# Two-layer recurrent and attention block: attention operands kept in DRAM as long rows per head, half-wide diagonal steps of two chunks joined, first transpose one step earlier

## The reference, cut to what matters

```python
# layer 1, B=4, S=2048, 16 heads, D_H=16, D_HR=8 (rotary), d_qk=24
Q = concat([Qc, rope(Qr)], -1)          # per head 16 + 8 rows
K = concat([Kc, rope(Kr)], -1)          # Kr is one set of 8 rows, the same for all heads
scores = clip(einsum('bhqd,bhkd->bhqk', Q, K), -80, 80)
scores = where(causal, scores, -inf)
weights = softmax(scores / sqrt(d_qk), axis=-1)
attn = einsum('bhqk,bhkd->bhqd', weights, V)
x = x + (attn @ W_O) * g                # g from the second gate
```

## Time and profile before

| | |
|---|---|
| median of three runs | 2309.38 us (2303.23 to 2310.4) |
| profiled execution, own time | 2303.42 us |
| its span | 2301.7 us |
| mean granted TensorE clock | 0.957 |
| busy, share of the span | PE 88%, DVE 76%, ACT 69%, PEld 39%, POOL 36% |
| DMA | 150477 packets, 165.72 MB, of which 127104 packets under 2 KB |

### The profile page before, as it was taken

How to read it: one execution, slowest core, us unless ns; L and a number is a source line. 1 busy time by engine, 2 the same in 40 slices (tenths; PEclk the granted TensorE clock), 3 DMA queues, 4 the chain that set the end, 5 groups by cost and what they waited for, 6 DMA issues and landing times. The chain is left out here.

```text
span 2301.7 us, 45469 instructions
## 1 busy us (share of the span) xinstructions
PE 2031.1 (88%) x18726; PEld 894.3 (39%) x18726; DVE 1740.6 (76%) x2557; ACT 1592.7 (69%) x1897; POOL 830.4 (36%) x653
## 2 busy tenths in 40 slices
PE   5999999999986887877988898999888999888987
PEld 2656556565653554554222222222222222222225
DVE  7776675766649999997778677888677887677777
ACT  5545464554535555555889898999888998888982
POOL 2635455354555666674111111111111111111108
PEclk9999999999997899898999999999999999999999
DMA  3001001010113434448343144442244432444228
GB/s 95 19 19 37 19 19 37 19 38 19 52 32 122 162 125 157 141 135 196 41 63 41 36 58 65 63 62 35 47 65 63 48 51 39 63 63 61 67 96 305
DMA packets 150477, 165.72 MB, mean 72 GB/s; under 512 B 12416, under 2 KB 127104, under 8 KB 150016
## 3 DMA queue, kind: packets, MB, share of 16 engines
q1 hardware_dynamic: 148240, 160.59, 32.6%
q10 hardware_dynamic: 2032, 2.24, 0.3%
HBM read 91.21 MB, written 71.57 MB: 71 GB/s over the span
## 5 line engine op out<-in xcount | busy, mean ns | idle before, releaser
L1635 DVE TENSOR_SCALAR c_probs<-c_probs 128x512 f32<-128x512 f32 (+3 forms) x1152 | 777.7, 709 | 268.0 <-ACT c_probs L1604 180.2
L1604 ACT ACTIVATE c_probs<-c_ps_b 128x1536 f32<-128x1536 f32 (+1 forms) x576 | 827.4, 1436 | 0.0
L1685 PE MATMUL c_ps_o<-c_probs,c_v 128*32 128x512 f32 (+3 forms) x5120 | 606.0, 551 | 69.3 <-issue 39.7
L1650 POOL TENSOR_SCALAR_AFFINE_SELECT c_probs<-c_probs 128x512 f32<-128x512 f32 x256 | 192.8, 764 | 952.1 <-DVE c_probs L1635 952.1
L1669 PE MATMUL c_ps_b<-c_qk 24*128 24x512 f16 (+3 forms) x5760 | 468.6, 353 | 23.6 <-issue 23.6
L1669 PE MATMUL c_ps_a<-c_qk 24*128 24x512 f16 (+3 forms) x1920 | 458.5, 350 | 33.8 <-ACT c_probs L1602 23.6
L1602 ACT ACTIVATE c_probs<-c_ps_a 128x512 f32<-128x512 f32 (+1 forms) x576 | 357.8, 621 | 127.1 <-PE c_ps_b L1669 127.0
L1669 PEld LDWEIGHTS c_ps_a<-c_qk 24*128 24x128 f16 x1920 | 140.0, 93 | 540.7 <-ACT c_probs L1604 346.4
L258 POOL TENSOR_TENSOR a_hidh<-a_hid,a_hidh 128x512 f16<-128x512 f32 x128 | 169.0, 1338 | 234.9 <-ACT a_hidh L356 231.0
L1685 PEld LDWEIGHTS c_ps_o<-c_probs,c_v 128*32 128x32 f32 x5120 | 109.5, 109 | 322.7 <-issue 142.3
L667 PE MATMUL a_ps<-a_xnh,a_w 128*128 128x512 f16 x768 | 172.0, 379 | 12.0 <-ACT a_hid L351 12.0
(11 more groups left out here) (242 smaller groups left out, 2884.8 us busy)
## 6 DMA issues: line engine op xcount, KB each, us to landing
v_d<-b_val SPq DMA_DIRECT2D x16, 1024.0 KB
c_v<-v_d SPq DMA_DIRECT2D x16, 1024.0 KB
rows<-in_x SPq DMA_DIRECT2D x16, 512.0 KB, 4.9
x_d<-rows_out SPq DMA_DIRECT2D x16, 512.0 KB, 3.2
rows<-x_d SPq DMA_DIRECT2D x16, 512.0 KB, 5.3
qc_d<-b_qc SPq DMA_DIRECT2D x32, 256.0 KB
kc_d<-b_kc SPq DMA_DIRECT2D x32, 256.0 KB
gate_d<-rows_out SPq DMA_DIRECT2D x16, 512.0 KB, 3.3
```

Of the source, the lines that this page charges most:

```text
L1604: nc.scalar.activation(probs[:, t % NPROB, PARTS[1], 0:width(t)], ps_b[:, t % 2, :, 0:width(t)], ACT.Exp, scale=unscale).then_inc(exp_b_do ...
L1635: nc.vector.tensor_scalar(tile, tile, P_MAX, P_MIN, ALU.min, ALU.max).then_inc(clip_done, 1)
L1650: pool.affine_select(out=tile, in_=tile, compare_op=ALU.is_ge, fill=0.0, base=0, pattern=[[0, GH], [1, P]], channel_multiplier=-1).then_in ...
L1685: mm = nc.tensor.matmul(ps_o[j * VW:(j + 1) * VW, first_query:first_query + w], v[:, kt, j * VW:(j + 1) * VW], probs[:, t % NPROB, j, at:a ...
```

## The change

1. **Layout in DRAM.** q and k go to one tensor `qk_d` [batch, head, 32 rows, q/k, half, 2048 tokens], so that a row of a head is 16 KB in one piece. Content rows are stored with four DMAs for q and four for k (by half and by block of 128 channels), the rotary rows of q with two, and those of k with two that write the same 8 rows for all 16 heads (a broadcast source). Values go to [batch, group, partition, key tile, 128], so that a partition's 8 KB of a group lie together. Stores per chunk: 13 in place of 7.
2. **Loads of a group.** Five DMAs in place of 17: one for each head (24 rows of 16 KB), one for the values (128 rows of 8 KB).
3. **Attention output.** `attn_d` becomes [head, 32 rows, tokens]. One DMA of 128 partitions stores a chunk (256 KB in place of 4 x 32 KB, rows without meaning included). The output stage loads each chunk with two DMAs, whose source is 8 heads x 16 rows and whose destination is 128 partitions.
4. **Steps.** The half-wide D2 steps of chunks 0 and 1 are joined to one step of full width, those of 2 and 3 likewise, so a group has 34 steps and there are 544. A joined step is the last of the even chunk. Its first half is multiplied by V in its own `values`; its second half belongs to the odd chunk and is multiplied in the `values` of the next step. The `probs` buffer of a joined step is therefore free one step later, and ACT waits for that (`consumed`).
5. **Order.** DVE takes the four tasks of a chunk one step earlier: ahead of the clips of e+2, e+3, e+4 and e+5. All steps have two clips of full width, as the full-width ones had before.

```diff
-        "qc": dram("qc_d", [BATCH, 2, DIM, SEQ], F16),
-        "qr": dram("qr_d", [BATCH, 2, HEADS * D_R, SEQ], F16),
-        "kc": dram("kc_d", [BATCH, 2, DIM, SEQ], F16),
-        "kr": dram("kr_d", [BATCH, 2, D_R, SEQ], F16),
-        "v": dram("v_d", [TOKENS, HEADS * VW]),
+        "qk": dram("qk_d", [BATCH, HEADS, VW, 2, 2, SEQ], F16),
+        "v": dram("v_d", [BATCH, GROUPS, P, KEYT, GH * VW]),
...
-        "attn": dram("attn_d", [DIM, TOKENS]),
+        "attn": dram("attn_d", [HEADS, VW, TOKENS]),
...
-                        sp.dma_start(d["qc"][b, h, :, t].rearrange("(m p) t -> p m t", p=P), qc[:, s, h]).then_inc(stored[s], 16)
+                        for m in range(KT):
+                            sp.dma_start(content[b, m, :, 0:D_H, 0, h, t], qc[:, s, h, m]).then_inc(stored[s], 16)
                     sp.wait_ge(kr_low, n + 1 + 1)
-                    sp.dma_start(d["kr"][b, :, :, t].rearrange("h p t -> p h t"), kr[:, s]).then_inc(stored[s], 16)
+                    for h in range(2):
+                        sp.dma_start(rotary[b, D_H:D_QK, :, 1, h, t],
+                                     kr[:, s, h:h + 1].to_broadcast([D_R, HEADS, CH])).then_inc(stored[s], 16)
...
+    for j in range(GH):
+        sp.dma_start(into.memory[VW * j:VW * j + D_QK], d["qk"][b, g * GH + j, 0:D_QK]).then_inc(into.loaded, 16)
+    sp.dma_start(into.v[:], d["v"][b, g]).then_inc(into.loaded, 16)
...
-    return t.rearrange("(k p) (n t) -> n p k t", p=P, t=CH)
+    return t.rearrange("(k e) r (n t) -> n k e r t", k=KT, t=CH)[:, :, :, 0:D_H]
...
+        at = len(fulls) // 2
+        return [(D0, TPC * c)] + fulls[:at] + [(D13, TPC * c)] + fulls[at:]
+
+    for g in range(BATCH * GROUPS):
+        for c in range(0, CPB, 2):
+            steps += [(g, c, kind, kt) for kind, kt in chunk_steps(c)]
+            steps += [(g, c, D2, TPC * c)]
+            steps += [(g, c + 1, kind, kt) for kind, kt in chunk_steps(c + 1)]
...
+            return [(c, kt + 2, 0, HALF, HALF), (c + 1, kt + TPC + 2, HALF, HALF, HALF)]
+        return [(c, kt, 0, CH, 0)]
+
+    def products(t):
+
+        now = pieces(t)[:1] if steps[t][2] == D2 else pieces(t)
+        if t and steps[t - 1][2] == D2:
+            return [(t,) + p for p in now] + [(t - 1,) + pieces(t - 1)[1]]
+        return [(t,) + p for p in now]
...
+    def consumed(t):
+
+        return t + 2 if steps[t][2] == D2 else t + 1
...
-                        act.wait_ge(pv_done, t - NPROB + 1)
+                        act.wait_ge(pv_done, consumed(t - NPROB))
...
-                for t in range(N + LAG + 4):
-                    for after, task in ((0, to_tokens), (1, reciprocal), (2, normalise), (3, to_channels)):
-                        if t - LAG - after in end_of:
-                            task(end_of[t - LAG - after])
+                for t in range(N + LAG + 3):
+                    for after, task in ((-1, to_tokens), (0, reciprocal), (1, normalise), (2, to_channels)):
+                        if t - LAG - after in end_at:
+                            task(end_at[t - LAG - after])
...
+                    for step, c, kt, at, w, first_query in products(t):
+                        e = g * CPB + c
+                        opens = len(opened) == e
+                        if opens:
+                            opened.append(t)
+                            if e:
+                                pe.wait_ge(tok_done, e)
```

More of the change, by code:

```diff
@@ L1492, in attention @@
     FULL, D0, D13, D2 = range(4)
[L1493 removed]
     def chunk_steps(c):
         fulls = [(FULL, kt) for kt in range(TPC * c)]
[L1498 to L1503 removed]
+        at = len(fulls) // 2
+        return [(D0, TPC * c)] + fulls[:at] + [(D13, TPC * c)] + fulls[at:]
+    steps = []
+    for g in range(BATCH * GROUPS):
[3 more added lines that the diff above has]
+            steps += [(g, c + 1, kind, kt) for kind, kt in chunk_steps(c + 1)]
     N = len(steps)
[L1505 to L1508 removed]
     LAG = 3
@@ L1514, in attention @@
     PARTS = (slice(0, 1), slice(1, GH))
+    HALF = CH // 2
     def pieces(t):
-        _, c, kind, kt = steps[t]
+        g, c, kind, kt = steps[t]
         if kind == D13:
-            return [(kt + 1, 0, CH - P, P), (kt + 3, CH - P, P, CH - P)]
+            return [(c, kt + 1, 0, CH - P, P), (c, kt + 3, CH - P, P, CH - P)]
         if kind == D2:
-            return [(kt + 2, 0, CH - 2 * P, 2 * P)]
-        return [(kt, 0, CH, 0)]
-    def width(t):
-        return CH - 2 * P if steps[t][2] == D2 else CH
-    diagonals = {FULL: (), D0: (0,), D13: (0, CH - P), D2: (0,)}
+            return [(c, kt + 2, 0, HALF, HALF), (c + 1, kt + TPC + 2, HALF, HALF, HALF)]
[5 more added lines that the diff above has]
+        return [(t,) + p for p in now]
+    ordered = [(steps[t][0], p[1], t) for t in range(N) for p in products(t)]
+    chunks = BATCH * GROUPS * CPB
+    end_of = {}
+    for g, c, t in ordered:
+        end_of[g * CPB + c] = t
+    ends = [end_of[e] for e in range(chunks)]
+    end_at = {t: e for e, t in end_of.items()}
+    assert len(end_at) == chunks
+    def consumed(t):
+        return t + 2 if steps[t][2] == D2 else t + 1
+    diagonals = {FULL: (), D0: (0,), D13: (0, CH - P), D2: (0, HALF)}
     masks = [0]
@@ L1663, in scores @@
                         pe.wait_ge(exp_a_done, t)
-                    for kt, at, w, first_query in pieces(t):
+                    for c, kt, at, w, first_query in pieces(t):
                         for i, (hk, hq) in enumerate(TERMS):
@@ L1753, in batch_stored @@
         def batch_stored(batches):
[L1755 removed]
+            return 16 * (batches * GROUPS * CPB // ahead.OUTS) + 16
         with nc.Block() as block:
@@ L1764, in _ @@
                 for s in range(ROWS, SLOTS):
-                    sp.dma_start(attn(s), attn_v[s]).then_inc(loaded[s], 16)
+                    for k in range(KT):
+                        sp.dma_start(attn(s)[:, k], attn_v[s, k]).then_inc(loaded[s], 16)
                 for s in range(ahead.OUTS):
```

89 lines of the change are left out of this document (36 added, 53 removed).

## The result

| | before | changed |
|---|---|---|
| median of the runs | 2309.89 us (2303.23 to 2312.94, 4 runs) | 2269.67 us (2265.95 to 2273.54, 4 runs) |
| ratio, 95% interval | | 0.983 [0.9803, 0.9857] |
| profiled execution, span | 2301.7 us | 2264.2 us |
| mean granted clock | 0.957 | 0.968 |
| DMA | 150477 packets, 165.72 MB | 118090 packets, 178.00 MB |

The account below looks back on a forecast made before the run. ACT, closely followed by PE, bounds the attention, with long idles when load bursts delay PE's instructions. Terms -70 - 2 + 11 + 3 = -58 us against 2303.4 gave 2245; half of a 6 us offset made it 2248, range 2200 to 2292.

Parts of the forecast that it names:

- What bounds the kernel: Attention: ACT leads PE by some 0.05 us a step; long idles, 89 us, come from PE's instruction fetch behind load bursts.
- Part 1: Group loads in attention: faster q/k and value transfers shorten the bursts, saving 70 us (0 to 89).
- the 20 us kept for the bursts that still hurt: Attention: of 89 us of long idles, 20 were assumed to remain, for the bursts latest to recover.
- Part 2: Attention steps: two fewer steps a group, offset by new waits at joined steps; -2 us in all (bounds -45 to +45).
- the first pair: First joined step of a group: DVE late with clips, masks and transpose, so ACT idles 2.3 us, against 1.27 in the second.
- the drift I had named: Attention: a drift of 0.01 to 0.02 us a step, given for most of the gap between computed and profiled stage time.
- my check of the stage: Attention: 16 groups of 64.9 us plus 89 us of idle give 1127, against 1149 us profiled.
- Part 3: Output stage: the attention load from 8 heads runs at half rate, 1.36 us more for each of 8 chunks, +11 us.
- Part 4: Stores of the projections: hidden until the last chunk, whose stores must land before the stage ends; +3 us (0 to 30).
- The sign that I had named for being wrong here: Projections: a stage longer than 386 us by more than 3 would show the forecast wrong.
- (a) to (d): Bursts stay as long, chance 0.12; values wait makes it slower, 0.08; everything hidden, 0.12; loads outlast the double buffer, 0.04.
- (a): Rival on the attention's group loads: bursts stay as long, only some 10 us of idle go, 2305 us; chance 0.12.

Follow-up runs that it names:

- e6: Kernel before, old layout, with a group's operand loads issued in four parts after successive chunks instead of all at once: 2218.73 us, ratio 0.9662.
- e8: Kernel before with q and k in 16 KB rows and the new attention output layout, values still in 512 B pieces: 2246.69 us, ratio 0.9781.
- f5: Changed kernel with the rotary rows of k stored once, so a head is loaded with three DMAs, not one: 2362.35 us, 1.0253 of the kernel before.
- e4: Changed kernel with DVE's transpose and the tasks behind it back at their old place, one step later: 2280.74 us, 0.9941 of the kernel before.
- e7: Kernel before with only the values in long rows of 8 KB: 2304.68 us, ratio 1.0028.
- e3: Changed kernel with five probability buffers in place of four and one x1 row fewer held ahead: 2234.66 us, 0.9701 of the kernel before.
- e5: Changed kernel with the attention's output in DRAM, its stores and its load as before: 2267.82 us, 0.9852 of the kernel before.
- f3: Kernel before's layout with joined steps, early transpose, five probability buffers and spread loads, first prefetched group included: 2188.39 us, ratio 0.9511.
- f4: Changed kernel with a group's loads spread over four chunks, the first prefetched group's too: 2249.28 us, 0.9781 of the kernel before.
- e1: Changed kernel's new DRAM layout with the 36 steps and task order of before: 2251.45 us, 0.9786 of the kernel before.

## Why the prediction was right or wrong

- **What bounds the kernel: right.** PE starves when a load burst stays slow for long. e6, e8 and f5 show it from three sides: cut short, shortened, and made long again. The reading behind it, instructions whose fetch stands behind the loads, was an inference; the q8 packets show it. The figure with it was wrong. I had counted 13 to 15 us from the burst's start; counted from the last q8 packet, PE mostly lasts 17 to 20 us. In e4 a burst began at 1581.8, 9.3 us after such a packet, and PE stopped already 8.8 us into it, for 3.7 us.
- **Part 1, -70 us: -69 measured** (excess 91.6 to 22.9), **partly by luck.** The rate, put at 150 GB/s, is 136 to 184. But the slow part, put at 10 to 12 us, took 15, and the whole burst 21 in place of some 15: in those 15 us some 2.4 MB moved, more than the 1.5 MB of q and k that I had priced. And the 20 us kept for the bursts that still hurt had no sum behind them; the same loads left 17.0 to 42.3 us in the other kernels. The reason given, more partitions in a DMA, stands beside the smaller number of DMAs (f5). The values' rows, which I had priced at a part of the gain, bring nothing (e7). The rule quoted from the Trainium skill, "SBUF — State Buffer", section "Door 1: The DMA port swizzle", agrees in direction with f5: 24 rows of a head at 136 to 184 GB/s, 16 and 8 rows at 82 to 135. It does not fix the size: the 117 GB/s of the old burst is above what it would give for four of 16 ports (an estimate of 109 GB/s by that page's 435), where I had taken the 85 alone as agreement.
- **Part 2, -2 us: +9 measured, and the step that failed is the conversion of idle into time.** The idles came out as worked: 1.26 + 1.20 in the first pair against 2.3, 1.19 in the second against 1.27, together 3.65 against 3.6. But three intervals of a group are longer by 1.51, 1.33 and 1.54 us, 4.4 in all, since a waiting exponential loses the 0.3 us by which it would have overlapped the one before it. I had added idles to 1.80 us a step. That is 0.7 us a group, 12 us. (Both groups are longer than I had them, 65.60 against 64.9 and 66.17 against 64.8; the drift I had named explains the first 0.7 of each. It does not explain all of the 22 us that my check of the stage had left: 11 are drift, some 3 more excess, 2 lie ahead of the first exponential and most of the rest behind the last.) In the first pair the place was half right: the chain of late transpose, clips and D13's masks is there, yet what stands behind it is values(D13), not the transpose that values(u+1) waits for; that wait has its plain 1.2 us like the other (e3 takes it away and leaves the mask's). "The transpose frees `ps_o` on time" was right, but e4 shows it to be worth 0.7 us a group with joined steps, which I had put at nothing.
- **Part 3, +11 us: +15.5 measured.** The period is 5.8 us against my 5.4; e5 gives the 15 us back. The term was undersized: half rate for the attention's 0.5 MB adds 1.36 us a chunk, 1.76 is what it costs. The rule of the Trainium skill, "DMA: Bandwidth & Descriptors", section on why a DMA increments its semaphore by 16, by which a source of 8 heads is moved by 8 DMA engines, fits in direction: the share of the DMA engines fell from 1.08 to 0.81. No row shows the number of engines.
- **Part 4, +3 us: +6.4 measured**, and about as much in every kernel that stores q and k in the new rows with the copies (1093.7 to 1096.1, against 1087.8 to 1089.2; 1091.3 in f5, without the copies). The sign that I had named for being wrong here, a projection stage longer by more than 3 us, came: 392 us for 386. The mechanism was the last chunk's stores, as said; the four k stores that hold SP for 6.70 us were not foreseen at 0.3 to 0.5 us a store.
- **The sum.** 2, 3 and 4 missed by 11, 4.5 and 3.4 us, all to the same side; with part 1 right that is 19 of the 22 us. The rivals (a) to (d) did not happen, though f5, with long rows in smaller pieces, has the long bursts that (a) describes, and more excess than before (118.6 us).

## What to carry to other kernels

When an in-order engine stands on "issue" during prefetches, look at the DMA queues of kind "instruction": a packet that comes late, and lands just before the engine goes on each time, shows what it waits for. Then look at how long the DMA engines stay busy without a break, and cut the prefetch into parts with time between them: that took a few lines and gained 80 us, where the new layout gained 52. Price a wait by the start-to-start interval of its engine's instructions, not by the idle in the profile, wherever neighbours overlap. When steps are merged so that a buffer is held longer, add the buffer in the same change: neither was worth anything alone here.

## What the runs showed of the hardware

- PE's instructions come as 16 KB packets in a DMA queue of their own, and they wait behind loads in the others: one every 10 us or so in quiet stretches (median interval 10.5 us before, from 1150 to 2180 us), up to 25 us apart across a burst. PE mostly lasts 17 to 20 us on what it has (12.5 at the least, some 30 in the first group), and goes on 1.2 to 1.9 us after the packet has landed (69 of 69).
- The harm of a long burst outlasts PE's idle. In f5 the granted clock was 0.60 and 0.54 in the two windows after the standstill, which is mostly the level of 1.2 GHz, and ACT was busy 2.66 of 4 us in the second. So part of the 91.6 us of excess of the kernel before is slow clock, not idle; over the attention its mean granted clock was 0.96, in the changed kernel 0.99.
- Long rows do not make DMAs into 16 and 8 partitions fast: 82 to 135 GB/s in windows of a burst with rows of 16 and 8 KB (f5), where rows of 4 KB had 117 and 85.
- Not settled: how much a given burst costs. It depends on where the burst falls between two q8 packets: in f5 the long idles of ACT begin 13.8, 19.3, 15.6, 21.1 and 17.5 us after the starts of five successive bursts, and then again 13.8, 19.3, 15.6, 23.0 and 17.5. No run shifted this on purpose. The excess that the long-row bursts leave differs between kernels with the same loads (17.0, 18.9, 22.9, 37.9 and 42.3 us in e4, e1, the changed kernel, e3 and e5), and e3's own runs spread from 2230.81 to 2247.19 us, of which the profiled one was the slowest. With spread loads the spread is gone too: the six runs of f3 lie within 4.3 us, and f4's excess is 2.4.
